# Flamingo layers: routed results of layer 1 gathered and added on chip, or added in memory

## The reference

```python
x = x + tanh(g_xattn[1]) * L1_xattn(layernorm(x), ctx)
x = x + tanh(g_ffn[1])   * L1_ffn(layernorm(x))

def L1_ffn(z):                        # z: 4096 x 256, E = 8 experts, top 2
    scores = softmax(z @ gate_w.T)
    chosen = top_k(scores + gate_bias, 2)          # two experts per token
    routed = sum over the two: scores[chosen] * mlp(z, w1[e], w2[e], w3[e])
    return routed + mlp(z, sw1, sw2, sw3)          # shared by all tokens

def mlp(z, w1, w2, w3):               # 256 -> 512 -> 256
    return (silu(z @ w1.T) * (z @ w3.T)) @ w2.T
```

## Time and profile before

| | us |
|---|---|
| median of 3 runs | 3286.59 (3286.03 to 3286.89) |
| profiled execution | 3280.55 |
| its span, first to last instruction | 3278.9 |
| mean granted TensorE clock | 0.957 of full speed |

### The profile page before, as it was taken

How to read it: one execution, slowest core, us unless ns; L and a number is a source line. 1 busy time by engine, 2 the same in 40 slices (tenths; PEclk the granted TensorE clock), 3 DMA queues, 4 the chain that set the end, 5 groups by cost and what they waited for, 6 DMA issues and landing times. The chain is left out here.

```text
span 3278.9 us, 48512 instructions
## 1 busy us (share of the span) xinstructions
PE 2992.5 (91%) x18056; PEld 2417.1 (74%) x18056; DVE 2166.0 (66%) x3824; ACT 1764.9 (54%) x2746; POOL 1361.6 (42%) x1007
## 2 busy tenths in 40 slices
PE   6999999999999999999879779999999747999995
PEld 5888888888888888888779745555554446999984
DVE  5777777777777777776645567777776342666654
ACT  3555555555555555555445348888888412555541
POOL 2111111111111111111044348888877353799975
PEclk9999999999999999999989879999999867999997
DMA  8101010010101001000056354344431241477743
GB/s 261 33 10 33 10 39 11 14 36 17 30 14 36 11 16 33 10 22 7 34 186 219 122 170 120 117 120 121 122 98 34 65 165 66 155 232 231 232 148 122
DMA packets 211558, 288.91 MB, mean 88 GB/s; under 512 B 18451, under 2 KB 154290, under 8 KB 211344
## 3 DMA queue, kind: packets, MB, share of 16 engines
q1 hardware_dynamic: 200848, 257.12, 25.2%
q0 software_dynamic: 10496, 28.92, 2.6%
HBM read 204.38 MB, written 81.53 MB: 87 GB/s over the span
## 5 line engine op out<-in xcount | busy, mean ns | idle before, releaser
L301 POOL TENSOR_TENSOR a_w_stage<-a_w_stage,a_consts 128x256 f32<-128x256 f32 x64 | 39.5, 617 | 1231.2 <-PE a_scores L36 1197.0
L1657 POOL TENSOR_TENSOR c_pT_lo<-c_prob,c_pT_hi 128x1024 fp32r<-128x1024 f32 x192 | 456.3, 2383 | 113.7 <-ACT c_pT_hi L1740 109.6
L387 ACT ACTIVATE a_prob<-a_scores,a_neg_max 128x1024 f32<-128x1024 f32 x256 | 286.1, 1118 | 361.1 <-DVE a_neg_max L485 357.2
L485 DVE TENSOR_REDUCE a_neg_max<-a_scores 128x1 f32<-128x1024 f32 x256 | 310.1, 1211 | 108.6 <-PE a_scores L36 108.5
L380 ACT ACTIVATE a_pT_hi<-a_probT 128x512 fp32r<-128x512 f32 x512 | 279.1, 598 | 186.7 <-PE a_probT L724 186.6
L1852 DVE TENSOR_REDUCE c_neg_max<-c_max 128x2 f32<-128x1024 f32 x248 | 302.2, 1218 | 70.4 <-PE c_max L2085 69.2
L432 DVE TENSOR_TENSOR a_pT_lo<-a_probT,a_pT_hi 128x512 fp32r<-128x512 f32 x512 | 327.5, 681 | 20.8 <-ACT a_pT_hi L380 20.8
L1734 ACT ACTIVATE c_prob<-c_scores 128x1024 f32<-128x1024 f32 x256 | 261.1, 1020 | 71.0 <-PE c_scores L2096 67.8
L724 PE MATMUL a_probT<-k_ident,a_prob 128*128 128x128 f32 x2048 | 268.5, 273 | 17.6 <-DVE a_pT_lo L432 17.6
L34 PE MATMUL m_h<-m_rT_hi,m_w_hi 128*128 128x256 f32 x880 | 258.4, 294 | 17.4 <-issue 8.9
L36 PE MATMUL m_h<-m_rT_hi,m_w_lo 128*128 128x256 f32 x880 | 254.7, 289 | 11.4 <-issue 11.3
(11 more groups left out here) (337 smaller groups left out, 8660.9 us busy)
## 6 DMA issues: line engine op xcount, KB each, us to landing
m_w_in<-L_ffn_w_in SPq DMA_DIRECT2D x117, 512.0 KB
e_w_in<-L_ffn_w_in SPq DMA_DIRECT2D x32, 1024.0 KB, 7.6
qk_dram<-c_stage SPq DMA_DIRECT2D x64, 256.0 KB
c_q_rows<-qk_dram SPq DMA_DIRECT2D x32, 512.0 KB, 5.0
c_k_rows<-qk_dram SPq DMA_DIRECT2D x32, 512.0 KB, 5.6
rows_in_dram<-a_zero SPq DMA_DIRECT2D x1, 10240.0 KB, 37.5
m_row_in<-rows_in_dram SPq DMA_DIRECT2D x39, 256.0 KB, 5.2
rows_out_dram<-m_res SPq DMA_DIRECT2D x39, 256.0 KB, 4.1
```

The costliest lines, as they stand in the source:

```text
L387: a(prob[:, qt, :], ps_s[:, qt % 2, :], ACT.Exp, bias=neg_max[:, qt:qt + 1], accum_out=row_sum[:, par, qt:qt + 1]).then_inc(exp_done, 1)
L485: ve.tensor_reduce(neg_max[:, qt:qt + 1], ps_s[:, qt % 2, :], AX.X, ALU.max, negate=True).then_inc(max_done, 1)
L1657: g.tensor_tensor(flat(pT[1][:, kt - 1]), flat(prob[:, kt]), flat(pT[0][:, kt - 1]).bitcast(F32), ALU.subtract).then_inc(lo_pool, 1)
```

## The change

- The order of tiles becomes 16 shared tiles (`NA` = 16), then 39 routed ones. All tiles split hidden values in the way of the shared ones (`hidden_high` on ScalarE, `hidden_low` on VectorE).
- A row of `z`, of `rows_in` and of `row_in` is now 258 numbers wide (`WIDE`): 256 values, the number of the token as an integer, and the factor of this choice. The 32 scatters of the first choice carry the first factor. VectorE then, in tile 5 and after those have landed, copies the second factors into `z`, and the 32 scatters of the second choice follow.
- A routed tile's result is multiplied by the factor of its rows and added in memory: `add` on GpSimd issues two indirect transfers with an addition (`compute_op=ALU.add`) that take the token numbers out of the rows. Their target is `sums`, a table of 4096 + 256 rows in memory. The shared tiles' results, with x, are stored there before (`keep`). Each tile's pair waits for the landing of the pair before it. Rows without a pair carry token numbers from 4096 on (`blank`), which the fill at the kernel's start writes.
- At the end, four copies of 1 MB go from `sums` to the output, within memory. The gathers, the additions on VectorE and the stores of rows are gone.
- `acc` is now the tile into which the gate loads x, so its eight loads fall away. The shared weights are loaded and their high parts made in the gate's blocks. The gate's sums over experts are one product and one reduction, and the row number's base is added once for both choices.
- SyncE's loop over routed tiles is written out.

```diff
-        for table in tables:
-                wide = table.rearrange("(p k r) d -> p k (r d)", p=P, r=1024 // D)
-                dma(wide, zero[:]... ).then_inc(cleared, 16)
+            wide = tables[0].rearrange("(p k r) d -> p k (r d)", p=P, r=1024 // D)
+            dma(wide, zero[:]... ).then_inc(cleared, 16)
+            sp.wait_ge(blank_set, 2)
+            wide = tables[1].rearrange("(j p t) d -> p j (t d)", p=P, t=RT)
+            dma(wide, blank[:]... ).then_inc(cleared, 16)
...
+            for j in range(3):                       # gate's block, SyncE, after the loads of x
+                view = ffn.shared_views[j]
+                nc.sync.dma_start(ffn.w_in[:, 0, j]..., view).then_inc(...)
...
-            then(ve.memset(base[:, 0:1], 0.0))
-            for e in range(E1):
-                then(ve.tensor_tensor(ends[:, e:e + 1], base[:, e:e + 1], tiles_of[:, e:e + 1], ALU.add))
-                if e < E1 - 1:
-                    then(ve.tensor_copy(base[:, e + 1:e + 2], ends[:, e:e + 1]))
+            then(ve.tensor_tensor(ahead_tiles[:], ahead[:], mid_axis(tiles_of[:], E1), ALU.mult))
+            then(ve.tensor_reduce(base[:], ahead_tiles[:], AX.X, ALU.add))
+            then(ve.tensor_scalar(base_row[:], base[:], float(R1), None, ALU.mult))
+            then(ve.tensor_tensor(place[:], place[:], mid_axis(base_row[:], NT), ALU.add))
...
-        NA = 10
+        NA = B * S // R1
+        SIDES = 6
...
             def load_rows(n):
                 j = n - NA
+                if j >= SIDES:
+                    sp.wait_ge(summed, 16 * RT * (j - SIDES + 1))
+                dma(row_in[:, j % SIDES]..., in_v[:, j]).then_inc(row_load[n % 2], 16)
+            def keep(n):
+                sp.wait_ge(o_out, n + 1)
+                dma(sums_v[:, n], acc[:, tokens(n)]).then_inc(kept, 16)
...
+            sp.wait_ge(summed, 16 * RT * NR)
+            for i in range(0, B * S, B * S // 4):
+                part = slice(i, i + B * S // 4)
+                dma(out_rows[part]..., sums[part]...).then_inc(out_stored, 16)
...
+            def add(n):                              # GpSimd
+                pool.wait_ge(o_out, n + 1)
+                if n == NA:
+                    pool.wait_ge(kept, 16 * (NA + 1))
+                else:
+                    pool.wait_ge(summed, 16 * RT * (n - NA))
+                for t in range(RT):
+                    at = row_in[:, (n - NA) % SIDES, t, D:D + 1].bitcast(I32)
+                    nc.gpsimd.indirect_dma_start(sums, bass.IndirectOffsetOnAxis(ap=at, axis=0), res[:, n % 2, t, :], None,
+                                                 bounds_check=B * S + R1 - 1, oob_is_err=True, compute_op=ALU.add).then_inc(summed, 16)
             for i in range(NT):
-                for c in range(TOP):
-                    scatter(i, c)
-                if i in (NT // 4, NT // 2):
-                    low(1, i // (NT // 2))
+                scatter(i, 0)
+            pool.wait_ge(second_weight, 1)
+            for i in range(NT):
+                scatter(i, 1)
+            for j in range(2):
+                low(1, j)
+            for n in range(NA, LAST + 1):
+                if n < LAST:
+                    low(number(n + 1), 0)
+                    low(number(n + 1), 1)
+                if n >= NA + 2:
+                    add(n - 2)
+            add(LAST - 1)
+            add(LAST)
...
             def result(n):                           # VectorE
                 dve.wait_ge(o_full, n + 1)
                 if routed(n):
                     if n >= NA + 2:
-                        dve.wait_ge(stored[n % 2], 16 * (places(n) // 2))
-                    ve.tensor_copy(flat(res[:, n % 2]), flat(ps_o[:, n % 2])).then_inc(o_out, 1)
+                        dve.wait_ge(summed, 16 * RT * (n - NA - 1))
+                    for t in range(RT):
+                        of_row = row_in[:, (n - NA) % SIDES, t, D + 1:D + 2]
+                        last = ve.tensor_scalar(res[:, n % 2, t, :], ps_o[:, n % 2, t, :], of_row, None, ALU.mult)
+                    last.then_inc(o_out, 1)
...
+                if n == 5:
+                    dve.wait_ge(scattered, 16 * NT)
+                    ve.tensor_copy(z[:, :, D + 1:D + 2]..., weight[:]).then_inc(second_weight, 1)
```

More of the change, by code:

```diff
@@ L2218, with layer1_gate @@
 FT1 = F1 // P
[L2221 removed]
+WIDE = D + 2
+def layer1_gate(nc, x3_dram, result_mv, wg_d, bias_d, K, tg, z, acc, ffn, rows, weight, tile_expert):
     with ExitStack() as ctx:
@@ L2310, in _, with __init__, sem, layer1_experts @@
             then(ve.tensor_scalar(tile_expert[:], found[:], float(E1 - 1), None, ALU.min))
[L2312 to L2316, removed]
-                then(ve.scalar_tensor_tensor(rows[:, c, :], offset[:], float(R1), rank[:], ALU.mult, ALU.add))
-def layer1_experts(nc, K, x3_dram, w1_d, w3_d, w2_d, shared, z, rows, weight, tile_expert, tg, rows_in, rows_out, out_dram):
+class SharedWeights:
+    def __init__(self, nc, ctx, shared):
+        def sem(name):
+            return ctx.enter_context(nc.semaphore("m_" + name))
+        self.w_in = ctx.enter_context(nc.sbuf_tensor("m_w_in", [P, 2, 3, DC * F1], F32))
+        self.w_high = ctx.enter_context(nc.sbuf_tensor("m_w_hi", [P, 2, 3, DC * F1], F32R))
+        self.w_load, self.w2_load = [sem("w_load0"), sem("w_load1")], [sem("w2_load0"), sem("w2_load1")]
+        self.w_hi = sem("w_hi")
+        self.shared_views = [v.rearrange("(c p) f -> p c f", p=P) for v in shared]
+def layer1_experts(nc, K, w1_d, w3_d, w2_d, ffn, z, acc, rows, weight, tile_expert, tg, rows_in, sums, out_dram):
     with ExitStack() as ctx:
@@ L2500, in _ @@
-            for b in range(B):
-                fetch(b)
+            def add(n):
[8 more added lines that the diff above has]
+                                                 bounds_check=B * S + R1 - 1, oob_is_err=True, compute_op=ALU.add).then_inc(summed, 16)
@@ L2531, in hidden_high @@
                 a(hT[0][:, n % 2, f], g[:, f], ACT.Copy).then_inc(h_act, 1)
-            def shared_tile(n):
+            rows_hi(0)
+            for n in range(LAST + 1):
+                m = number(n)
+                ahead = routed(n) and n < LAST
+                if ahead:
+                    split(m + 1, 0)
                 silu(n, 0)
@@ L2543, in shared_tile @@
                 hidden_high(n, 3)
-            split(0, 0)
-            split(0, 1)
-            rows_hi(0)
-            split_w2(0)
-            for n in range(NA):
-                shared_tile(n)
+                if routed(n):
+                    split_w2(m)
                 if n == 0:
@@ L2628, in add @@
-            def add(b):
-                for c in range(TOP):
-                    for t in range(TB):
-                        i = TB * b + t
-                        if c == 0 and t % RT == 0:
-                            j = i // RT
-                            dve.wait_ge(o_out, (j if j < NA else j + NR) + 1)
-                        if c == 0 and t == 0:
-                            dve.wait_ge(fetched[b % 2], 16 * GROUP * (b // 2 + 1))
-                        if c:
-                            dve.wait_ge(added, GROUP * b + t + 1)
-                        ve.scalar_tensor_tensor(acc[:, i], parts[:, b % 2, t, c], weight[:, c, i:i + 1], acc[:, i], ALU.mult, ALU.add).then_inc(added, 1)
@@ L2641, in add_last @@
-            def add_last():
-                dve.wait_ge(o_out, LAST + 1)
-                for t in range(TB):
-                    i = NT - TB + t
-                    dve.wait_ge(last_fetched[t], 16 * TOP)
-                    for c in range(TOP):
-                        if c:
-                            dve.wait_ge(added, GROUP * (B - 1) + TOP * t + 1)
-                        ve.scalar_tensor_tensor(acc[:, i], parts[:, (B - 1) % 2, t, c], weight[:, c, i:i + 1], acc[:, i],
-                                                ALU.mult, ALU.add).then_inc(added, 1)
```

278 lines of the change are left out of this document (107 added, 171 removed).

## The result

| | before | changed |
|---|---|---|
| median | 3286.31 us (3279.41 to 3286.89, 4 runs) | 3251.06 us (3249.36 to 3252.75, 4 runs) |
| profiled execution | 3280.55, span 3278.9 | 3252.75, span 3251.1 |
| mean granted clock | 0.957 | 0.962 |

What follows compares the result with a forecast made beforehand. TensorE, busy 91% of the span, was taken as the bound, so only its losses in layer 1's feed-forward part could be won. Terms -3.5 - 6 - 24 - 30.5 + 3 + 0 + 1 = -60 took 3286.6 to 3227 us, range 3195 to 3290.

Steps and rivals of the forecast that it cites:

- part 1: Gate's chain before layer 1's experts: five small operations replace a memset and fifteen steps, products and reductions go; -3.5 us.
- part 2: Start of the experts' block: shared weights read earlier, first matmul after about 3.5 us instead of 9.5; -6 us.
- part 3: Scattering beside shared tiles: two runs of 32 scatters cut TensorE's loss to 33 us; -24 us, bounds -36 and 0.
- the 34 that the prediction named as a sign of being wrong: Second scattering run: a TensorE loss as large as 34 us, its upper bound, would show the forecast wrong.
- the end at "0" of its bounds: Scattering: the unfavourable bound of the forecast gain, 0 us, where the two runs win nothing.
- parts 4 and 5: Routed tiles: moving six shared tiles ahead removes the tail's loss, -30.5 us; 78 adding transfers stay hidden, +3 us.
- part 6: After the last matmul: last pairs 9.3 us, copies 21.2 plus 2 for completion; change 0, bounds -12 and +6 us.
- my two ends: Copies at the end: 10.6 us at the loads' rate, or 21.2 if each byte counts once read and once written.
- part 7: Layer 0's fill at the kernel's start: shorter rows may delay later loads; +1 us, bounds 0 and +6.
- The second (the number of transfers counts): Routed tiles: the stall follows the number of indirect transfers, not their runs; 3268 to 3294 us, chance 0.14.
- The third (slow additions): Routed tiles: slow adding in memory makes each pair wait; 3360 us if landing takes 10 us, chance 0.14.
- The fourth (two runs starve as much as one): Scattering: two runs starve TensorE as much as one did, so that step gives 0; 3251 us, chance 0.12.

Runs made afterwards that it cites:

- x11_splits_back_third: Changed kernel with GpSimd's two weight splits back among the first run's scatters, on a stalling chip: 3233.35 us, ratio 0.9850 to the kernel before.
- x7_five_per_tile_again: Changed kernel with the same 64 scatters spread, five per shared tile, on a stalling chip: 3188.51 us, ratio 0.9705 to the kernel before.
- x1_splits_back: Changed kernel with GpSimd's two weight splits back among the first run's scatters, on a fast chip: 3179.18 us, ratio 0.9916 to the kernel before.
- x2_five_per_tile: Changed kernel with the 64 scatters spread, five per shared tile, on a fast chip: 3180.82 us, ratio 0.9915 to the kernel before.
- x8_add_into_output: x2_five_per_tile with sums kept in the output tensor and no copies at the end, on a fast chip: 3165.71 us, ratio 0.9865 to the kernel before.
- x4_rows_of_272: Changed kernel with table rows of 272 numbers instead of 258, on a fast chip: 3183.99 us, ratio 0.9925 to the kernel before.

## Why the prediction was right or wrong

**The gate's chain (part 1): right in size, not to be seen in the total.** From the sum over tiles at 2640.92 the chain took 9.45 us to its end at 2650.37; it now takes 6.04, from 2644.37 to 2650.41: -3.4. The block still starts at 2650.4, since everything before the chain ran 3.5 us later. That belongs to the changed kernel and not to this one execution: the last routing step of layer 0 (`route_w`) starts at 1647.9 to 1649.4 in the three traces of the kernel before and its variant, and at 1650.4 to 1654.5 in all eleven of the changed kernel and its variants, on both kinds of chip. It is spread evenly (from the third on, a batch of layer 0 takes 199.8 us instead of 199.4), in a part that the change hardly touches. I did not find its cause, and the prediction put it at nothing.

**Shared weights in the gate's block (part 2): right.** 3.0 us to the first matmul instead of the forecast 3.5.

**The scatters (part 3): the step that failed.** It forecast a new loss of 33 us (10.7 and 20 beside the two runs, 2.6 behind) and so -24; the loss is 70.5 (34.4 and 36.1) and the difference +13.2. The kind of event, its place and its end behind the run are as described, but "the second run starts after a rest, so it is bounded by 10.7 (like the first)" took the first 41 us of the kernel before as an unbroken run. They are not one. The two weight splits stand in the scattering, the first within these 41 us and the second in the 50 behind, in GpSimd's timeline of the kernel before:

```profile
2677.64 2.37 POOL L2469 TENSOR_TENSOR m_w_lo<-m_w_in,m_w_hi 128x1024 fp32r<-128x1024 f32 x1 [1.92 <-ACT m_w_hi L2509]
...
2700.40 2.37 POOL L2469 TENSOR_TENSOR m_w_lo<-m_w_in,m_w_hi 128x1024 fp32r<-128x1024 f32 x1
```

TensorE stalled from 2671.3 to 2677.4, ran until 2689.5, stalled until 2702.2, ran until 2707.6, and stalled to the end: it came free each time within 2 us of the start of a pause. With 180 matmuls in the window to 2692.0 against 77 in the next 50 us, I read a stall that grows late, where it was a stall cut short twice by pauses; "the 12 us for which TensorE ran free in the first" were the time behind a pause. The change takes both pauses out, which I counted as nothing. x11_splits_back_third puts them back and regains 16 of the 37 us of the miss; x7_five_per_tile_again breaks up both runs and regains 61, all but some 9 of the loss. The second run, at 36, also passed the 34 that the prediction named as a sign of being wrong, and the end at "0" of its bounds was too near: it excluded a loss for no reason that a row gave. One thing stays open: in the kernel before the first stall came 20 us after the first scatter, in the changed kernel 13, and behind its second pause TensorE ran free for 5 us only.

**The tiles behind (parts 4 and 5): the six tiles right, the agreement to 0.1 us luck.** -27.6 against -27.5, but made up otherwise. The tail's loss was 29.0, not 30.5, by the end of the last matmul. A tile takes 9.005 us where it took 9.073, in all variants of the changed kernel alike, which brings some 3.1 us that I did not foresee and cannot explain. And some 4.5 us (an estimate: 418.8 less 414.3 at this rate) are lost, where I put 3 for TensorE stalling with "issue" beside the adding transfers. Nearly nothing of that kind shows; what shows is a wait for rows from memory, four times, which I had not counted (waits of PE, 2805 to 3224.5):

```profile
PE m_t L2681 <- DMA m_row_in<-rows_in_dram: 2.5, 4, 0.9
PE m_o L34 <- issue: 0.8, 1, 0.8
```

So the routed tiles are not starved by GpSimd's 78 transfers: TensorE is busy for 361.48 of 364.80 us in their window. VectorE was undersized: 6.2 us a tile forecast, 311.6 / 364.8 x 9.0 = 7.7 measured, still hidden. The groups of VectorE's instructions in the routed window (busy us, mean ns, idle before) show the term:

```profile
L2580 DVE TENSOR_TENSOR m_hT_lo<-m_g,m_hT_hi 128x256 fp32r<-128x256 f32 x160 | 159.7, 998 | 11.5 <-ACT m_hT_hi L2549 6.7 <-issue 1.1
```

and in the shared tiles from 2786.5, where GpSimd does nothing:

```profile
L2580 DVE TENSOR_TENSOR m_hT_lo<-m_g,m_hT_hi 128x256 fp32r<-128x256 f32 x32 | 13.4, 420 | 1.4 <-ACT m_hT_hi L2549 0.2
```

The same instruction takes 0.42 us alone and 1.00 beside GpSimd's splits. I had priced it from shared tiles.

**The end (part 6): the mechanism was right, the copies were mis-sized.** The pairs cost a little more than forecast (3.6 to 3.8 us to land behind the issue, not 3.0, and 1.85 us from one issue to the next, not 1.31): from the last matmul to the last landing 11.3 us, not 9.3. The copies take 3251.1 - 3235.7 = 15.4 us with their completion, not 21.2 + 2: 4.19 MB in 15.4 us are 272 GB/s each way at the least. It lies between my two ends. The Trainium skill, "DMA: Bandwidth & Descriptors", section "Latency and other measured facts", gives 214 GB/s per direction as full for copies of tiles between tensors in memory, an estimated 19.6 us; the measurement, in 128 packets of 32 KB, is faster, and it decides.

**The fill (part 7): as bounded.** 38.9 us to landing instead of 37.5; TensorE shows no wait for it.

**The rivals.** The second (the number of transfers counts) fell twice: 78 more of them cost nothing visible beside the routed tiles, and x7_five_per_tile_again has the same 64. The third (slow additions) fell: issue and landing of a pair take 6.4 us, from 3217.39 to 3223.78, and a tile 9.0. The fourth (two runs starve as much as one) came nearest: its 3251 is the measured median. That is luck in part, since its sum is another: the scattering lost 13 more than before, the end gave 7 of it back, and the rest is the profiled execution of the kernel before, which was quicker than its median.

## What to carry to other kernels

Before a bound is read from a window of the old trace, list what stands in it besides the thing to be priced; here two small instructions of another kind kept the stall short, and the edit took them out. Indirect transfers of this size issued back to back for more than 6 to 8 us should be broken by other work, or spread over tiles, which showed no cost on a fast chip (3181 us against 3179 to 3184 of the other variants) and gained 61 us on one that stalls. When a forecast line agrees to a tenth of a us, check that its terms do too. When a cost has no releaser in the profile, run the old kernel on more than one chip before believing that it belongs to the program.

## What the runs showed of the hardware

**The stall comes and goes with the chip, or with something else that is fixed for a set of runs.** The same program takes 3207 to 3209 us in two sets of runs and 3283 to 3286 in three, always the one or the other within a set, and the variants follow: x1_splits_back 3179 and 3182 against 3233 (51 to 54 more), x2_five_per_tile 3181 against 3189 (8 more), x8_add_into_output 3166 against 3173 (7 more), the kernel before 74 to 79 more. The spread versions hardly care which chip they get. What differs between the chips stays open. The changed kernel itself, and longer rows beside a stall (x4_rows_of_272), were not run on both kinds, so whether row length matters in a stall is undecided too.

**What TensorE lacks in a stall is not the next block of instructions.** While it runs freely, the queue "q8 instruction" moves a packet of 16 KB every 14 to 16 us, and 137 of them over the execution, which fits TensorE's 36,112 matmuls and weight loads at 256 a packet (141). The DMA view of the changed kernel from 2661 to 2706 (queue, kind: packets, MB, share) has the whole first hole and 9 us of free running behind it, and no packet of that queue; the second fence is from 2706 to 2750:

```profile
q0 software_dynamic: 1357, 3.72, 22.7%
q1 hardware_dynamic: 1081, 1.31, 8.2%
q14 instruction: 1, 0.01, 0.1%
```
```profile
q1 hardware_dynamic: 1090, 1.05, 7.0%
q0 software_dynamic: 288, 0.79, 5.1%
q8 instruction: 3, 0.05, 0.4%
```

TensorE came out of the hole at 2697 without a new block, so what it issued next must have been there already (an inference, with that queue taken as TensorE's by its count). The Trainium skill, "Runtime: NRT & Kernel Launch", section "Instruction fetch mechanics", says that blocks of 16 KiB are fetched ahead and the crossing mostly hidden; the packets agree with that, and this speaks against a late block of instructions as the cause. Inside the hole the instructions come in steps, as TensorE's timeline shows (start, us, what, idle before), first near its beginning, then near its end:

```profile
2666.49 0.28 PE L35 MATMUL m_h<-m_rT_lo,m_w_hi 128*128 128x256 f32 x1 [1.14 <-issue]
2667.21 0.28 PE L36 MATMUL m_h<-m_rT_hi,m_w_lo 128*128 128x256 f32 x1 [0.43 <-issue]
2667.91 0.36 PE L2681 MATMUL m_t<-k_ident,z 128*128 128x128 f32 x1 [0.43 <-issue]
2668.62 0.37 PE L2681 MATMUL m_t<-k_ident,z 128*128 128x128 f32 x1 [0.36 <-issue]
...
2692.67 0.37 PE L36 MATMUL m_h<-m_rT_hi,m_w_lo 128*128 128x256 f32 x1 [2.43 <-issue]
2694.10 0.37 PE L34 MATMUL m_h<-m_rT_hi,m_w_hi 128*128 128x256 f32 x1 [1.05 <-issue]
```

It is 0.7 us from one to the next, or twice that before the first. From 2678 on the distances are 0.7, 1.4, 2.1 or 2.8 us, all near multiples of 0.7 (2.8 before the line at 2692.67, 1.4 behind it), while a scatter takes 1.28 from start to start: the steps don't follow the scatters one by one. The mechanism behind them is open; no run here separates it further.

**VectorE beside GpSimd.** The 0.42 and 1.00 us above are one operation with two inputs in on-chip memory. The Trainium skill, "SBUF — State Buffer", section "SBUF: two separate sides", says that such an operation and a GpSimd operation that reads this memory exclude each other for the whole instruction; the stretching agrees, and VectorE's operations with one input from the matmuls' memory (m_rT_lo, 0.69 us in the shared stretch, 0.68 in the routed one) were not stretched.
